# Recommender attention kernel: PE's waits for two pooled banks, in the first round of products, moved apart

## What is computed

```python
outer = jnp.einsum('bi,bnj->bnij', candidate_ad, goods).reshape(Bs, Ns, Ks * Ks)
k_b = jnp.broadcast_to(candidate_ad[:, None, :], (Bs, Ns, Ks))
h1 = jnp.concatenate((k_b, goods, outer), axis=-1)
act = jax.nn.sigmoid(h1 @ W1 + b1)          # 36 hidden values a row
weight = act @ W2 + b2
out = jnp.sum(goods * weight, axis=1)       # (2048, 32)
```

## Time and profile before

| | |
|---|---|
| runs | 262.2, 262.45, 263.8 us; median 262.45 us |
| profiled execution | 262.6 us, of which the span of the profile is 260.8 us |
| granted TensorE clock, mean | 0.992 |
| share of the span: PE, ACT, DVE | 95%, 86%, 80% |
| pairs in the loop | 60, one in about 3.57 us |

### The profile page before, as it was taken

One profiled execution on the slowest core, in us unless ns is written; L12 is line 12 of the kernel. 1 busy time (PEld: TensorE's weight loads), 2 busy tenths in 40 slices (PEclk: granted clock), 3 DMA queues, 4 the chain that ended last, 5 costly groups with the idle time before them and its releaser, 6 DMA issues.

```text
span 260.8 us, 18353 instructions
## 1 busy us (share of the span) xinstructions
PE 248.3 (95%) x7492; PEld 133.6 (51%) x7492; DVE 209.6 (80%) x1176; ACT 224.3 (86%) x658; POOL 147.0 (56%) x285
## 2 busy tenths in 40 slices
PE   6997989999999999999999999999999999999970
PEld 2335545455555555555555555555555555555540
DVE  0892568679888889888888888898888898888896
ACT  2898978978999999999999999999999999999940
POOL 1300664646766566665666666656666566665562
PEclk9999999999999999999999999999999999999996
DMA  5991876767778787777778887877777877887100
GB/s 209 284 322 29 248 221 181 224 189 232 242 225 239 224 225 237 234 238 227 223 221 244 227 249 207 239 232 240 229 233 224 230 237 233 238 230 224 53 1 10
DMA packets 38243, 55.10 MB, mean 211 GB/s; under 512 B 4256, under 2 KB 37920, under 8 KB 38048
## 3 DMA queue, kind: packets, MB, share of 16 engines
q1 hardware_dynamic: 37920, 54.41, 70.5%
q10 hardware_dynamic: 288, 0.32, 0.3%
HBM read 54.45 MB, written 0.26 MB: 210 GB/s over the span
## 4 chain that ended last, share of the span: by engine, by line
PE 87%; ACT 7%; DVE 2%; DMA 2%; issue 1%; ACTq 0%; DVEq 0%
PE w_ps L394 28%; PE z_ps L349 25%; PE x_ps L370 16%; PE w_ps L430 6%; PE x_ps L430 6%; PE s_ps L349 4%; ACT wm L485 4%; DMA act<-w_outer 2%; DVE goods L557 2%; ACT act L506 2%; ACT wxd L485 1%; PE z_ps L300 0%; ACT actx L514 0%; DVE whole L550 0%; PE z_ps L430 0%
## 5 line engine op out<-in xcount | busy, mean ns | idle before, releaser
L506 ACT ACTIVATE act<-z_ps,bias 128x200 f32<-128x200 f32 x384 | 129.4, 440 | 20.5 <-PE z_ps L349 10.9
L349 PE MATMUL z_ps<-goods,wm_ring 32*32 32x200 f32 x3072 | 80.3, 340 | 2.6 <-issue 1.2
L268 POOL TENSOR_TENSOR rest<-whole,top 128x200 f32<-128x200 f32 x64 | 36.3, 567 | 59.5 <-DVE top L552 35.9
L557 DVE CUSTOM_DVE_ANT_0 goods<-w_ps,goods 128x200 f32<-128x200 f32 x122 | 39.8, 364 | 30.8 <-PE z_ps L430 16.0
L394 PE MATMUL w_ps<-act,consts 128*32 128x200 f32 x1024 | 56.6, 339 | 0.7 <-ACT actx L514 0.7
L370 PE MATMUL x_ps<-goods,wx 128*32 128x200 f32 x1024 | 55.4, 333 | 0.0
L270 POOL TENSOR_SCALAR mid<-rest,consts 128x200 bf16<-128x200 f32 x64 | 50.3, 785 | 6.3
L349 PEld LDWEIGHTS z_ps<-goods,wm_ring 32*32 32x32 f32 x3072 | 30.3, 103 | 34.4 <-issue 33.0
L557 DVE CUSTOM_DVE_ANT_0 goods<-z_ps,goods 128x200 f32<-128x200 f32 x140 | 44.9, 361 | 0.0
L506 ACT ACTIVATE act<-s_ps,bias 128x200 f32<-128x200 f32 x128 | 44.9, 461 | 0.0
L246 POOL COPY wx<-wxd 32x96 f32<-32x96 f32 (+1 forms) x88 | 22.8, 259 | 37.0 <-PE x_ps L370 22.8
(11 more groups left out here) (45 smaller groups left out, 233.1 us busy)
## 6 DMA issues: line engine op xcount, KB each, us to landing
goods<-goods_t SPq DMA_DIRECT2D x256, 200.0 KB, 2.8
act<-cand_r SPq DMA_DIRECT2D x1, 1024.0 KB, 5.4
act<-cand_u SPq DMA_DIRECT2D x1, 256.0 KB, 3.0
candb<-cand_b SPq DMA_DIRECT2D x1, 256.0 KB, 3.8
out_t<-out_stage SPq DMA_DIRECT2D x4, 64.0 KB, 3.1
consts<-small ACTq DMA_DIRECT2D x1, 164.5 KB, 5.4
act<-w_outer ACTq DMA_DIRECT2D x1, 144.0 KB, 5.6
pick_sb<-pick SPq DMA_DIRECT2D x1, 128.0 KB, 3.5
```

What stands on the lines that cost most here:

```text
L268: nc.gpsimd.tensor_tensor(rest[:, :], whole[:, q % 2, :], top[:, q % 2, :], ALU.subtract).then_inc(part_step, 1)
L349: last = nc.tensor.matmul(z_bank(slot, r)[32 * c:32 * c + 32, N * s:N * s + N], wm_ring[32 * r:32 * r + 32, slot % RING, 4 * s + c, :], go ...
L506: last = nc.scalar.activation(act[:, p % A_SLOTS, r, N * s:N * s + N], z_bank(p, r)[:, N * s:N * s + N], ACT.Sigmoid, bias=bias[:, r, p, s ...
L557: one = nc.vector.tensor_tensor_reduce(goods[:, q % G_SLOTS, v, :], s_banks(q, f)[s][:, N * i:N * i + N], goods[:, q % G_SLOTS, v, :], 1.0 ...
```

## The change

The two waits that stood together ahead of tile row 2 are pulled apart. The one for pooled01 goes to the head of the first round. The one for pooled11, with `pick_loaded`, goes from tile row 2 to tile row 3, so that it stands ahead of the last four tiles instead of the last eight. Nothing is computed otherwise. It holds for slots 4 and up, which are the 60 pairs of the loop.

```diff
                         pe.wait_ge(z_read, p)
+                    if slot >= LAG + 1:
+
+                        pe.wait_ge(pooled[0][1], p)
                 for r in range(4):
-                    if s == 0 and r == 2 and slot >= LAG + 1:
+                    if s == 0 and r == 3 and slot >= LAG + 1:
 
                         pe.wait_ge(pick_loaded, 16)
-                        pe.wait_ge(pooled[0][1], p)
                         pe.wait_ge(pooled[1][1], p)
```

## The result

| | median us | runs |
|---|---|---|
| before | 262.6 | 22 |
| after | 264.18 | 22 |

The ratio is 1.0048, with a 95% interval of 1.0027 to 1.0068: the change costs 0.7 to 1.8 us, about 1.3. (Ratios here are estimated from all runs of both kernels, so they need not be the quotient of the medians, which lie 1.6 us apart.) That is a small loss, but one that this many runs can tell from none. The profiled execution of the changed kernel has a span of 262.6 us against 260.8.

A forecast was written before the change was run, and what follows sets the result against it. The prediction took PE, through its time per pair, as the bound. Its terms 0.3 + 0.0 + 0.0 = +0.3 us on a median of 262.45 gave 262.7 us, rounded down, with a range of 261.2 to 264.3 us (chance 0.82).

The forecast's parts named there:

- What bounds the kernel: PE alone forms the chain of waits; 60 pairs at 3.57 us are 214 of the 260.8 us.
- The inner wait: First round, moved from tile row 2 to 3: +0.005 us a pair, +0.3 us in all; both banks already free.
- the hole: First round: pause of about 0.075 us in tile starts at the inner wait, the price of passing the instruction.
- the term for the hole: Inner wait ahead of tile row 3: nearly the same pause as before, +0.005 us a pair, +0.3 us in all.
- The bound, +0.03 us from slot 3's late last tiles: First round, upper limit: PE's queue runs short deeper in the round, at most +0.03 us a pair, +1.8 us.
- The lower bound: First round: four more tiles' starts cover part of the pause, -0.02 us a pair, -1.2 us.
- sign for a wrong hole: Profile after, first round: `spread` at +0.57 us, or at +0.65 us and more, instead of +0.63 to +0.64.
- The head: First round's head: pooled01 is up in time, the second wait instruction is hidden in 0.61 us of cover; 0.0 us.
- The first (the hole goes): First round falls to 0.57 or 0.56 us, 3.6 to 4.2 us faster, 258.2 to 258.9 us; chance 0.06.
- The second (the head uses up the store): Two waits at the head leave no tiles ready: second pause of 0.075 us a pair, +4.5 us, 267.0 us; chance 0.05.
- The third (the bank was late): Tile row 2 had been waiting for pooled11; at row 3 the wait shortens, -1.8 us, 260.6 us; chance 0.07.
- The Trainium skill's queue: TensorE queue 64 entries deep: the inner wait's place would not matter, its term 0.0 instead of +0.3 us.

The follow-up runs named there:

- the wait for nothing: Kernel before plus a wait for long-ended loads in the second round: ahead of tile row 2 267.76 us (1.0171), ahead of row 3 268.39 us (1.0225).
- the half change: Against the changed kernel: pooled01's wait kept at the head, pooled11's put back ahead of tile row 2; 262.37 us, ratio to before 1.0002.

## Why the prediction was right, and what was off

**What bounds the kernel** held. PE is the whole chain in the middle of both traces, and every change in the length of a round came back in the time, 60-fold within the intervals: +0.024 us a pair as +1.3 us (0.7 to 1.8), -0.062 us as -4.5 us (3.3 to 5.8), +0.077 us as +4.5 (2.8 to 6.2).

**The inner wait.** That its two banks are free long before, and that the hole is the price of passing the instruction, was argued from the earlier trace rows and is now shown by the wait for nothing. That the hole moves behind tile 12 and the round's end follows the last tile is shown by the counts. What failed in size is the term for the hole: the forecast took it as nearly equal, +0.005 us a pair and +0.3 us in all, and it is +0.024 us, 1.3 to 1.4 us. An equal hole needs a wait whose turn comes four tiles' starts later, 4 x 0.007 = 0.028 us; in the traces its turn comes 0.054 us later, from +0.023 to +0.077. The 0.026 us between these two are the loss. The bound, +0.03 us from slot 3's late last tiles, was the right row to read, and its reason has the right sign: towards the round's end PE's queue has less in store. The lower bound had no row behind it. Taking a value near the middle gave that empty bound weight; the row that existed should have had it. By the prediction's own sign for a wrong hole, `spread` at +0.65 us or more, the hole was wrong: the median is 0.654 us, and the pair has 3.60 us where 3.57 to 3.58 was forecast.

**The head.** Its second wait instruction costs nothing, as forecast, now shown by itself. pooled01 there waits for nothing. Even pooled11 there would cost nothing.

**The rivals.** The first (the hole goes) did not happen with the change: the hole goes by moving the wait forward, and the round is as long with the wait behind fourteen tiles as behind twelve. The second (the head uses up the store) is refuted by the half change and, harder, by the kernel that stands at the head until 0.16 us before the round and still has 0.57 us. The third (the bank was late) is refuted, since a wait for nothing makes the same 0.630 us.

**The Trainium skill's queue** of 64 entries (page "TensorE: Matmul & The Clock Gate", section "Architectural detail: the array is 16× 32×32, not 1× 128×128") does not describe what hides a wait here. By it 24 and 32 array instructions (two loads and two matmuls a tile) would be alike, but a wait behind six tiles, 24 of them, is hidden and one behind eight, 32, is not.

The range held the time, and within 1% was right. But 264.18 us lies only 0.1 us under the range's upper end, 264.3, so that it held was partly luck. The sign of the small difference, a loss, was right too; the forecast size, 0.3 us, was a quarter of the measured 1.3.

**What stays open.** Why the store ends between six and eight tiles; why the wait's turn varies from pair to pair behind twelve tiles (+0.068 to +0.126 us, and the round's length with it) and behind eight does not; why the first round without a hole has 0.567 us and the second 0.553, with the last two tiles late even where nothing is waited for. No run here tells these apart.

## What to carry to other kernels

A wait that has long been satisfied is not free if it stands as an instruction of its own in the middle of a burst of short, parallel products: unless PE has taken it up before the burst begins, everything behind it starts late, and the burst ends with its last tile. Don't move such a wait later to let more tiles start; put it at the burst's head or among its first tiles, provided the semaphore comes while the engine is still busy with the stage before (here 0.16 us before the first tile was enough). To size it, put a wait for nothing at the place in question and read the burst's length.

## What the runs showed of the hardware

A wait instruction of PE between float32 tiles of 32 x 32 x 200 costs 0.00 us behind four or six of 16, 0.062 to 0.077 us behind eight, and 0.087 to 0.10 us behind twelve, whether it waits for one semaphore or two and whether they come from a register's value or a constant. With eight or more in front PE takes the wait up inside the burst, with four (0.134 and 0.294 us) or six (0.255 us) before it. The kernel with the wait ahead of tile row 1 differs from the one before by a single digit: 258.12 us against 261.83 in the same comparison.
